# Recurrence: four small LoRA products side by side in the array, and two scalings made by ScalarE

## The chip, the cores and the metric
One core of a Trainium2 chip. The metric is the device time of one execution in microseconds (us), the median of several executions.

## The reference, cut to what matters
Two feed-forward blocks stand around a recurrence ("attn") with 8 batches of 512 tokens and 128 channels, `LORA = 32`. What the change touches, from the recurrence:

```
xm = x + dxa * miu_x
lora_h = tanh(xm @ A_lora).reshape(b, t, 5, -1)
miu = lambda_ + einsum('btfi,fic->fbtc', lora_h, B_lora)
w_in, k_in, v_in, r_in, g_in = x[None] + dxa[None] * miu
y_t = r_t @ (S + u * k_t^T v_t);  S = diag(decay_t) S + k_t^T v_t
yn = groupnorm(y) * gn_gamma + gn_beta
return yn * g @ Wo.T
```

The second LoRA factor is a product with 32 rows of contraction for each of five inputs f (w, k, v, r, g). r times u is an operand of the recurrence's diagonal; the scale and the bias of the group norm are applied to its turned output.

## The kernel before
The program runs in phases, each ended by a barrier of all engines. The recurrence is one phase. It works batch by batch on 128 channels by 512 tokens, in fp32. Each engine has its own instruction stream, and semaphores of the class `Signal` (`wait` for a value made, `free` for a buffer given back) join them.

The parts of the work are named by kind. "mix" makes batch b+1's projections, "scan" does batch b's recurrence in levels of doubling length, "tail" normalises, turns and projects batch b-1, and "next" prepares batch b+2. All engines go through one written order, each taking the parts that it has. There is no planner.

```
ORDER = (("scan", "start"), ("mix", "lora"), ("tail", "norm"), ("scan", "level1"), ("mix", "shift0"),
         ("mix", "mixed0"), ("scan", "level2"), ("mix", "shift1"), ("tail", "turn"), ("mix", "mixed1"),
         ("scan", "level3"), ("mix", "shift2"), ("tail", "out"), ("mix", "td"), ("mix", "mixed2"), ("scan", "level4"),
         ("mix", "shift3"), ("mix", "rate"), ("scan", "level5"), ("mix", "shift4"), ("next", "xm"), ("scan", "far"),
         ("mix", "mixed3"), ("mix", "k"), ("scan", "keys"), ("mix", "mixed4"), ("mix", "v"), ("scan", "state"),
         ("mix", "r"), ("mix", "g"), ("mix", "chain"), ("mix", "first_k"), ("scan", "y"))
```

`batches` (L1476) runs this order once with mix alone, once without tail, then a hardware loop of two turns with two runs each, and four runs more. So there are eight runs with a mix part, eight with a scan part and eight with a tail part.

The lines that matter, by engine:
- TensorE: `mix_lora` (L1791, L1793) makes the first factor, whose tanh ScalarE writes to `lora` (L1705) and `lora4` (L1706). `mix_shift(f)` (L1810) makes the second factor of input f. For f below 4 it multiplies all 128 rows of `lora` by `B_lora[:, f, :]`, which is zero outside the 32 rows of f; for f = 4 it takes 32 rows. The results go to the PSUM banks 2, 3, 0, 1 and again 2. The scan levels are L1859 (64 rows by 32 columns), the far products L1880, `tail_turn` L1918, `tail_out` L1924, the projections td, k, r, g L1785, and rate L1820.
- VectorE: `mix_shift(f)` (L1538) adds lambda and multiplies by dxa. `keep_level` (L1642) copies a level's result under a mask, `next_q` (L1589) scales the queries. `mix_r` (L1546) makes `ru` = q0 times u, once ScalarE has copied r to q0. `mix_g` (L1552) makes the gate from ScalarE's tanh. `mix_chain` (L1566) makes the products of the decay. `tail_turn` makes `yg` = scale times the turned output plus bias (L1627), and then `ygT` = yg times gate (L1631), which `tail_out` on TensorE needs.
- GpSimd: `mixed` (L1662, five in a run), `next_k` (L1681, seven in a run), the group norm's power (L159) and scaling (L165).
- ScalarE: the PSUM copies k (L1730), the turned keys (L1761), seven copies into aT (L1767, L1771), v (L1734), r (L1738), the gate's tanh (L1743), and 14 copies of decay factors (L1755, L1756).

Of the kernel before, what the change touches and what calls it, by code (L numbers as in the profile page):

```python
# [8 lines left out]
ALU = mybir.AluOpType  # L9
ACT = mybir.ActivationFunctionType  # L10
# [1329 lines left out]
LORA = 32  # L1340
# [75 lines left out]
def recurrence_phase(nc, ps, s, x_all, zT):  # L1416
# [8 lines left out]
    with Phase(nc) as ctx:  # L1425
# [14 lines left out]
        dxa, xm, lora, lora4 = sb("dxa", [P, T]), sb("xm", [P, T]), sb("lora", [P, T]), sb("lora4", [LORA, T])  # L1440
# [76 lines left out]
        with nc.Block() as block:  # L1517
            @block.vector
            def _(vec):
                v = nc.vector  # L1520
# [10 lines left out]
                def mix_shift(f):  # L1531
                    def part(b, i):
                        miu_made.wait(vec, b, f + 1)
                        if f >= 2:
                            mixed_ready.wait(vec, b, f - 1)
                        else:
                            mixed_ready.free(vec, b)
                        v.scalar_tensor_tensor(shift[f % 2][:], ps[:, MIU_BANK[f], :], s["lambda"][:, f:f + 1], dxa[:],  # L1538
                                               ALU.add, ALU.mult).then_inc(shift_ready.sem, 1)
                    return part  # L1540

                def mix_r(b, i):
                    r_kept.wait(vec, b)
                    if not isinstance(b, int) or b >= 2:
                        level_made.free(vec, b - 1)
                    v.tensor_scalar(ru[i][:], q0[i][:], s["u"][:, 0:1], None, ALU.mult).then_inc(ru_kept.sem, 1)  # L1546

                def mix_g(b, i):
                    gt_kept.wait(vec, b)
                    if not isinstance(b, int) or b >= 2:  # L1550
# [71 lines left out]
                    gn.variance(vec, b)  # L1622

                def tail_turn(b, i):
                    yn_turned.wait(vec, b)
                    ygT_ready.free(vec, b)
                    v.tensor_scalar(yg[:], ps[:, YT_BANK, :], s["gn_w_half"][:, 0:1], s["gn_b_half"][:, 0:1], ALU.mult,  # L1627
                                    ALU.add).then_inc(yg_ready.sem, 1)
                    yg_ready.wait(vec, b)
                    out_made.free(vec, b)  # L1630
                    v.tensor_tensor(ygT[:], yg[:], gate[i][:], ALU.mult).then_inc(ygT_ready.sem, 1)  # L1631
# [7 lines left out]
                def keep_level(b, l):  # L1639
# [3 lines left out]
                                      ps[:, LEVEL_BANK:LEVEL_BANK + NH, 0:TPB * BLOCK].rearrange("p h (c w) -> p h c w", c=TPB)  # L1643
                                      ).then_inc(level_kept.sem, 1)

                batches(vec, next_xm=next_xm, **{f"mix_shift{f}": mix_shift(f) for f in range(5)}, mix_r=mix_r,
                        mix_g=mix_g, mix_chain=mix_chain, scan_start=scan_start, **{f"scan_level{l}": scan_level(l) for l in range(1, DIAG_LEVELS + 1)},
                        scan_far=scan_far, scan_state=scan_state, scan_y=scan_y,
                        tail_norm=tail_norm, tail_turn=tail_turn, tail_out=tail_out)
# [48 lines left out]
            @block.scalar  # L1698
            def _(act):
                a = nc.scalar  # L1700

                def mix_lora(b, i):
                    lora_made.wait(act, b)
                    miu_made.free(act, b)
                    a.activation(lora[:], ps[:, 0, :], ACT.Tanh).then_inc(lora_kept.sem, 1)  # L1705
                    a.activation(lora4[:], ps[0:LORA, 1, :], ACT.Tanh).then_inc(lora_kept.sem, 1)  # L1706

                def mix_td(b, i):
                    td_made.wait(act, b)
                    w_made.free(act, b)  # L1710
                    a.activation(td_hidden[:], ps[0:HS, TD_BANK, :], ACT.Tanh).then_inc(td_kept.sem, 1)

                def mix_rate(b, i):
                    w_made.wait(act, b)
                    decay_ready.free(act, b)
                    a.activation(rate[:], ps[:, W_BANK, :], ACT.Exp, bias=s["td_miu"][:, 0:1]).then_inc(rate_ready.sem, 1)
                    rate_ready.wait(act, b)
                    if not isinstance(b, int) or b >= 2:
                        factors.free(act, b - 1)
                        chain.free(act, b - 1)  # L1720
                    a.activation(decay[i][:], rate[:], ACT.Exp, scale=-1.0).then_inc(decay_ready.sem, 1)

                def mix_k(b, i):
                    k_made.wait(act, b)
                    if not isinstance(b, int) or b >= 2:
                        level_made.free(act, b - 1)
                        k_next.free(act, b - 1)
                        q_next.free(act, b - 1)
                        y_made.free(act, b - 1)
                    a.activation(k0[i][:], ps[:, K_BANK, :], ACT.Copy).then_inc(k_kept.sem, 1)  # L1730

                def mix_v(b, i):
                    v_made.wait(act, b)
                    a.activation(v_rows[i][:].rearrange("p c w -> p (c w)"), ps[:, V_BANK, :], ACT.Copy).then_inc(v_kept.sem, 1)  # L1734

                def mix_r(b, i):
                    r_made.wait(act, b)
                    a.activation(q0[i][:], ps[:, R_BANK, :], ACT.Copy).then_inc(r_kept.sem, 1)  # L1738

                def mix_g(b, i):  # L1740
                    g_made.wait(act, b)
                    g_kept.free(act, b)
                    a.activation(gate_tanh[:], ps[:, G_BANK, :], ACT.Tanh, scale=0.5).then_inc(gt_kept.sem, 1)  # L1743

                def mix_chain(b, i):
                    for l in range(LEVELS):
                        src = decay[i] if l == 0 else block_decay[l - 1]
                        pairs = src[:].rearrange("p (n two) -> p n two", two=2)
                        if l:
                            chain.wait(act, b, l)  # L1750
                        else:
                            decay_ready.wait(act, b)
                            q_next.free(act, b)
                            k_next.free(act, b)
                        a.activation(q_factor[l][:, :, 1], pairs[:, :, 0], ACT.Copy)  # L1755
                        a.activation(k_factor[l][:, :, 0], pairs[:, :, 1], ACT.Copy).then_inc(factors.sem, 1)  # L1756

                def scan_keys(b, i):
                    kT_made.wait(act, b)
                    kv_made.free(act, b)  # L1760
                    a.activation(kT[:].rearrange("p c w -> p (c w)"), ps[:, KT_BANK, :], ACT.Copy).then_inc(kT_kept.sem, 1)  # L1761
                    far_made.wait(act, b)
                    y_made.free(act, b)
                    bank = LEVEL_BANK
                    far = ps[:, bank:bank + NH, :].rearrange("p h (c t) -> p h c t", c=TPB)
                    for at, to in ((slice(0, 32), slice(32, 64)), (slice(64, 96), slice(96, 128)), (slice(0, 64), slice(64, 128))):
                        a.activation(aT[at, :, :, to], far[at, :, :, to], ACT.Copy).then_inc(far_kept.sem, 1)  # L1767
                    level_kept.wait(act, b)
                    for q in range(P // BLOCK):
                        at = slice(q * BLOCK, (q + 1) * BLOCK)  # L1770
                        a.activation(aT[at, :, :, at], diag[at, :, :, :], ACT.Copy).then_inc(near_kept.sem, 1)  # L1771

                def scan_y(b, i):
                    gn.squares(act, b)

                batches(act, mix_lora=mix_lora, mix_td=mix_td, mix_rate=mix_rate, mix_k=mix_k, mix_v=mix_v, mix_r=mix_r,
                        mix_g=mix_g, mix_chain=mix_chain, scan_keys=scan_keys, scan_y=scan_y)

            @block.tensor
            def _(pe):  # L1780
                t = nc.tensor
# [10 lines left out]
                    k_kept.free(pe, b)  # L1792
                    t.matmul(ps[0:LORA, 1, :], s["A_lora"][:, P:], xm[:], start=True, stop=True).then_inc(lora_made.sem, 1)  # L1793

                def mix_shift(f):
                    def part(b, i):
                        if f == 0:
                            lora_kept.wait(pe, b)

                            r_kept.free(pe, b)  # L1800
                            ru_kept.free(pe, b)
                        elif f == 1:
                            v_kept.free(pe, b)
                        elif f == 4:
                            shift_ready.wait(pe, b, 1)
                        if f == 4:
                            lhsT, rhs = s["B_lora4"][:], lora4[:]
                        else:
                            lhsT, rhs = s["B_lora"][:, f, :], lora[:]
                        t.matmul(ps[:, MIU_BANK[f], :], lhsT, rhs, start=True, stop=True).then_inc(miu_made.sem, 1)  # L1810
                    return part

                def mix_td(b, i):
                    shift_ready.wait(pe, b, F_K + 1)
# [106 lines left out]
                def tail_out(b, i):  # L1921
                    ygT_ready.wait(pe, b)
                    for c in range(TPB):
# [1 line left out]
                                        start=True, stop=True)  # L1925
                    last.then_inc(out_made.sem, 1)

                batches(pe, mix_lora=mix_lora, **{f"mix_shift{f}": mix_shift(f) for f in range(5)}, mix_td=mix_td,
                        mix_rate=mix_rate, mix_k=mix_k, mix_v=mix_v, mix_r=mix_r, mix_g=mix_g,
                        scan_start=scan_start, **{f"scan_level{l}": scan_level(l) for l in range(1, DIAG_LEVELS + 1)},  # L1930
                        scan_far=scan_far, scan_keys=scan_keys, scan_state=scan_state, scan_y=scan_y,
# [96 lines left out]
```

## Time and profile before
| | us |
|---|---|
| median of 3 runs | 1597.56 |
| lowest and highest of them | 1591.68, 1601.63 |
| the profiled execution, its own time | 1610.69 |
| its span, first to last instruction | 1608.9 |
| PE, DVE, ACT, POOL busy over the span | 1292.8, 1121.5, 877.7, 698.0 |
| TensorE's mean granted clock | 0.867 |

PE is TensorE's matmuls, PEld its weight loads, DVE VectorE, ACT ScalarE, POOL GpSimd. A busy time is a union of intervals. The granted clock is a share of full speed: 1.00 is 2.4 GHz, 0.50 is 1.2 GHz. The profile's own page cuts the span into 40 equal slices of 40 us, too coarse for the recurrence, which lies between about 685 and 955 us. The sections below therefore use its windows, its groups by line and its timeline.

### The profile page before, as it was taken

To read this page: it belongs to the slowest core of one execution; us is meant where nothing else is said; L and a number is where in the kernel's file an instruction comes from. 1 tells how busy PE (TensorE), PEld (TensorE's weight loads), DVE (VectorE), ACT (ScalarE), POOL (GpSimd) and SP (SyncE) were. 2 spreads that over 40 slices of the span, in tenths; PEclk is the share of its full clock that TensorE was granted. 3 is DMA by queue.
4 is the path that set the end of the run, shared out by engine and by line. 5 is a ranking of instruction groups with operands and counts; after the bars stand their busy time and mean duration, and the time that the engine had idled before them with its cause. 6 is when DMAs were issued, how large, how long until landed. Compare 5 with 4: busy or idle time off the path is not lost. (4 is left out here: it accounts for less than half of the span.)

```text
span 1608.9 us, 39937 instructions
## 1 busy us (share of the span) xinstructions
PE 1292.8 (80%) x12720; PEld 732.9 (46%) x12721; DVE 1121.5 (70%) x1736; ACT 877.7 (55%) x1782; POOL 698.0 (43%) x817
## 2 busy tenths in 40 slices
PE   3579999999978397278788745489999999976693
PEld 2324444434458397125445433234444444476593
DVE  7678888888736232758788759588889888463232
ACT  3438888888841153224334314168888888820351
POOL 5433333333336365246566625513333333336462
PEclk9769999999975599589899858689999999965797
DMA  3421433211100121100000002512111111001224
GB/s 111 167 57 43 112 91 78 62 49 48 29 1 30 48 68 51 41 2 2 3 2 2 3 1 105 150 36 51 45 54 46 48 53 45 12 1 43 62 68 117
DMA packets 81641, 81.93 MB, mean 51 GB/s; under 512 B 16265, under 2 KB 53868, under 8 KB 81536
## 3 DMA queue, kind: packets, MB, share of 16 engines
q1 hardware_dynamic: 72704, 70.01, 15.6%
q0 software_dynamic: 4608, 8.44, 1.6%
q10 hardware_dynamic: 4224, 2.10, 0.4%
q8 instruction: 64, 1.05, 0.3%
q14 instruction: 41, 0.34, 0.1%
HBM read 50.56 MB, written 29.93 MB: 50 GB/s over the span
## 5 line engine op out<-in xcount | busy, mean ns | idle before, releaser
L795 DVE TENSOR_REDUCE maxima<-ps 128x2 f32<-128x1024 f32 x512 | 624.1, 1226 | 88.1 <-PE ps L624 83.1
L777 ACT ACTIVATE probs<-ps 128x512 f32<-128x512 f32 x1024 | 553.1, 593 | 87.0 <-PE ps L651 69.7
L624 PE MATMUL ps<-k_stack,q_stack 62*128 62x512 f32 x1024 | 385.8, 476 | 36.6 <-DMA k_stack<-k_split 25.5
L651 PE MATMUL ps<-q_stack,k_stack 64*128 64x512 f32 x1024 | 390.0, 459 | 0.3
L661 PE MATMUL ps<-probs,v_stack 128*32 128x256 f32 x4096 | 327.5, 392 | 1.1 <-ACT probs L777 1.0
L590 POOL TENSOR_TENSOR inv<-o_rows,minus_one 128x16 f32<-128x16 f32 x64 | 186.3, 2911 | 237.4 <-ACT o_rows L758 237.4
L624 PEld LDWEIGHTS ps<-k_stack,q_stack 62*128 62x128 f32 x1024 | 157.7, 193 | 229.7 <-issue 115.9
L651 PEld LDWEIGHTS ps<-q_stack,k_stack 64*128 64x128 f32 x1024 | 159.3, 186 | 17.0 <-issue 7.3
L661 PEld LDWEIGHTS ps<-probs,v_stack 128*32 128x32 f32 x4096 | 80.9, 108 | 171.7 <-issue 112.2
L1275 POOL DMA_INDIRECT expert_out<-yt,number x80 | 78.7, 984 | 69.0 <-issue 44.4
L1233 ACT ACTIVATE xT<-ps,ln_b,ln_w 128x128 f32<-128x128 f32 x80 | 36.6, 458 | 107.2 <-PE ps L1204 105.1
L1252 DVE COPY w_now<-w 128x512 f32 x80 | 34.4, 430 | 77.8 <-issue 41.6
L1210 PE MATMUL ps<-xT,w_now 128*128 128x128 f32 x640 | 88.4, 283 | 0.1
L1217 PE MATMUL ps<-w,hidT 128*128 x640 | 84.9, 276 | 0.0
L1210 PEld LDWEIGHTS ps<-xT,w_now 128*128 128x128 f32 x640 | 80.6, 198 | 0.4 <-issue 0.3
L583 POOL CAST neg_wide<-maxima 128x16 fp32r<-128x16 f32 x64 | 12.7, 198 | 155.1 <-DVE maxima L795 155.1
L1217 PEld LDWEIGHTS ps<-w,hidT 128*128 128x128 f32 x640 | 78.4, 193 | 0.1
L1133 POOL DMA_INDIRECT sorted<-rows,slot x64 | 62.2, 972 | 26.5 <-issue 16.4
L1238 ACT ACTIVATE hidT<-ps 128x512 f32<-128x512 f32 x80 | 47.8, 598 | 36.4 <-PE ps L1210 35.8
L1681 POOL TENSOR_TENSOR r_kx<-r_kx,r_k_factor 128x512 f32<-128x512 f32 x48 | 60.6, 1263 | 13.0 <-PE ps L1859 9.6
L1662 POOL TENSOR_TENSOR r_mixed<-r_shift,zT 128x512 f32<-128x512 f32 x40 | 57.1, 1436 | 19.0 <-DVE r_shift L1538 19.0
L420 PE MATMUL ps<-hT,w_qkv 128*128 128x512 f32 x64 | 44.7, 837 | 17.4 <-ACT hT L384 17.4
(215 smaller groups left out, 1843.8 us busy)
## 6 DMA issues: line engine op xcount, KB each, us to landing
q_stack<-q_split SPq DMA_DIRECT2D x256, 64.0 KB
k_stack<-k_split SPq DMA_DIRECT2D x512, 32.0 KB
q_split<-q_parts SPq DMA_DIRECT2D x16, 512.0 KB, 2.8
k_split<-k_parts SPq DMA_DIRECT2D x16, 512.0 KB, 3.6
xt<-sorted SPq DMA_DIRECT2D x80, 64.5 KB
w<-in_L_ffn_w SPq DMA_DIRECT2D x16, 256.0 KB, 3.0
rows<-expert_out SPq DMA_DIRECT2D x16, 256.0 KB, 3.2
x_all<-in_L_attn_x SPq DMA_DIRECT2D x8, 256.0 KB, 3.0
```

The lines of the kernel that those rows point to most:

```text
L590: g_.tensor_tensor(inv[:], o_rows[:, :, :, DK], minus_one[:], ALU.pow).then_inc(inv_ready, 1)
L624: mm = t.matmul(psS[:, h, :], qs[g][score_rows(h), h // 2, u * P:(u + 1) * P], ks[g][score_rows(h), h // 2, :], start=True, stop=True)
L651: t.matmul(ring("e", u, n), ks[g][half(h), h // 2, u * P:(u + 1) * P], qs[g][half(h), h // 2, :], start=True, stop=True).then_inc(e_ready, 1)
L661: last = t.matmul(psO[VW * h:VW * (h + 1), here], vs[g][:, u, h, :], probs[u % 2][:, h, here], start=(u == 0 and part == 0), stop=(u == TP ...
L777: a.activation(probs[u % 2][:, h, :], ring("e", u, n), ACT.Exp, scale=float(DK) ** -0.5).then_inc(e_read, 1)
L795: v.tensor_reduce(maxima[i][:, :, pair, u:u + 1], psS[:, 2 * pair:2 * pair + 2, :], AX_X, ALU.max, negate=True).then_inc(s_read, 1)
L1133: pool.indirect_dma_start(xs, bass.IndirectOffsetOnAxis(ap=slot[:, i:i + 1], axis=0), rows[:, i, :], None).then_inc(scattered, 16)
L1210: last = t.matmul(psH[o][:, c * P:(c + 1) * P], w1_now[o][:, c * P:(c + 1) * P], xT[o][:], start=True, stop=True)
L1217: last = t.matmul(psY[i][:, 0:P], hidT[i][:, c, :], s["w2"][:, ds(second_expert, 1), c, :], start=(c == 0), stop=(c == HC - 1))
L1275: pool.indirect_dma_start(ys, bass.IndirectOffsetOnAxis(ap=number[out_slot][:], axis=0), yt[out_slot][:], None, bounds_check=TOK - 1, oob_ ...
L1662: g.tensor_tensor(mixed[f][:], shift[f % 2][:], x, ALU.add).then_inc(mixed_ready.sem, 1)
L1681: g.tensor_tensor(dst[:].rearrange("p (k m) -> p k m", m=m), src[:].rearrange("p (k m) -> p k m", m=m), k_factor[l][:].rearrange("p n two ...
```

## The change
TensorE's parts shift0 to shift3 become one part at shift0: four matmuls, each with the 32 rows of its own f of weights and of `lora`, one behind the other in the queue, to four different banks. They wait at the top for all that the four waited for. VectorE still takes shift0 to shift3 in their old places. VectorE's `ru` goes to ScalarE, from PSUM, behind the copy of r; VectorE's `yg` goes to ScalarE, from PSUM. The number of matmuls stays the same.

```diff
@@ VectorE
-                def mix_r(b, i):
-                    r_kept.wait(vec, b)
-                    if not isinstance(b, int) or b >= 2:
-                        level_made.free(vec, b - 1)
-                    v.tensor_scalar(ru[i][:], q0[i][:], s["u"][:, 0:1], None, ALU.mult).then_inc(ru_kept.sem, 1)
...
                 def tail_turn(b, i):
-                    yn_turned.wait(vec, b)
-                    ygT_ready.free(vec, b)
-                    v.tensor_scalar(yg[:], ps[:, YT_BANK, :], s["gn_w_half"][:, 0:1], s["gn_b_half"][:, 0:1], ALU.mult,
-                                    ALU.add).then_inc(yg_ready.sem, 1)
                     yg_ready.wait(vec, b)
                     out_made.free(vec, b)
                     v.tensor_tensor(ygT[:], yg[:], gate[i][:], ALU.mult).then_inc(ygT_ready.sem, 1)
@@ ScalarE
                 def mix_r(b, i):
                     r_made.wait(act, b)
                     a.activation(q0[i][:], ps[:, R_BANK, :], ACT.Copy).then_inc(r_kept.sem, 1)
+                    if not isinstance(b, int) or b >= 2:
+                        level_made.free(act, b - 1)
+                    a.activation(ru[i][:], ps[:, R_BANK, :], ACT.Copy, scale=s["u"][:, 0:1]).then_inc(ru_kept.sem, 1)
...
+                def tail_turn(b, i):
+                    yn_turned.wait(act, b)
+                    ygT_ready.free(act, b)
+                    a.activation(yg[:], ps[:, YT_BANK, :], ACT.Identity, bias=s["gn_b_half"][:, 0:1],
+                                 scale=s["gn_w_half"][:, 0:1]).then_inc(yg_ready.sem, 1)
@@ TensorE
+                def mix_shift0(b, i):
+
+                    lora_kept.wait(pe, b)
+                    r_kept.free(pe, b)
+                    ru_kept.free(pe, b)
+                    v_kept.free(pe, b)
+                    for f in range(4):
+                        at = slice(f * LORA, (f + 1) * LORA)
+                        t.matmul(ps[:, MIU_BANK[f], :], s["B_lora"][at, f, :], lora[at, :],
+                                 start=True, stop=True).then_inc(miu_made.sem, 1)
+
+                def mix_shift4(b, i):
+                    shift_ready.wait(pe, b, 1)
+                    t.matmul(ps[:, MIU_BANK[4], :], s["B_lora4"][:], lora4[:], start=True, stop=True).then_inc(miu_made.sem, 1)
```

## Rows read from the trace of the kernel before
**Rows 1.** Window: busy us (instructions) of PE, PEld, DVE, ACT, POOL; granted clock, DMA share, GB/s.
```profile
685.00:955.00 270.00, 210.28 (x4064) 123.65 (x4064) 202.50 (x344) 93.51 (x257) 150.86 (x130) 0.87 0.01 2
```

**Rows 2.** Groups by line, 685 to 960 us: count | busy, mean ns | idle before.
```profile
L1810 PE MATMUL ps<-r_lora,B_lora 128*128 128x512 f32 x64 | 40.8, 728 | 3.8 <-ACT r_lora L1706 3.8
...
L1627 DVE TENSOR_SCALAR r_yg<-ps,gn_w_half,gn_b_half 128x512 f32<-128x512 f32 x8 | 6.4, 801 | 4.8 <-PE ps L1918 4.8
...
L1716 ACT ACTIVATE r_rate<-ps,td_miu 128x512 f32<-128x512 f32 x8 | 5.5, 688 | 15.8 <-PE ps L1820 15.8
...
L1546 DVE TENSOR_SCALAR r_ru<-r_q,u 128x512 f32<-128x512 f32 x8 | 3.9, 487 | 7.1 <-ACT r_q L1738 7.1
```

**Rows 3.** Timeline of POOL, one ordinary run: start, us, what, count [idle before].
```profile
743.29 1.16 POOL L1681 TENSOR_TENSOR r_kx<-r_kx,r_k_factor 128x512 f32<-128x512 f32 x1
744.40 1.73 POOL L1662 TENSOR_TENSOR r_mixed<-r_shift,zT 128x512 f32<-128x512 f32 x1
746.10 1.09 POOL L1681 TENSOR_TENSOR r_kx<-r_kx,r_k_factor 128x512 f32<-128x512 f32 x1
...
753.51 1.05 POOL L1681 TENSOR_TENSOR r_kx<-r_kx,r_k_factor 128x512 f32<-128x512 f32 x1 [0.47 <-PE ps L1859]
```

**Rows 4.** Timeline of DVE, the same run.
```profile
740.87 0.68 DVE L1589 TENSOR_TENSOR r_qx<-r_qx,r_q_factor 128x512 f32<-128x512 f32 x1
...
743.67 1.33 DVE L1589 TENSOR_TENSOR r_qx<-r_qx,r_q_factor 128x512 f32<-128x512 f32 x1
...
753.62 0.44 DVE L1642 COPY_PREDICATED r_diag<-level_masks,ps 128x256 f32<-128x256 int32 x1 [0.83 <-PE ps L1859]
...
762.36 0.48 DVE L1546 TENSOR_SCALAR r_ru<-r_q,u 128x512 f32<-128x512 f32 x1 [0.70 <-ACT r_q L1738]
762.87 0.69 DVE L1552 SCALAR_TENSOR_TENSOR r_gate<-r_gate_tanh,ps 128x512 f32<-128x512 f32 x1
```

**Rows 5.** Timeline of PE, the same run.
```profile
742.83 0.28 PE L1859 MATMUL ps<-r_qx,r_kx 64*32 64x32 f32 x12 [0.79 <-issue]
...
755.26 0.68 PE L1880 MATMUL ps<-r_qx,r_kx 64*64 64x64 f32 x16 [0.40 <-DVE r_qx L1589]
755.87 1.13 PE L1785 MATMUL ps<-r_mixed,WkT 128*128 128x512 f32 x2
```

**Rows 6.** Timeline of ACT, the same run.
```profile
757.25 0.60 ACT L1730 ACTIVATE r_k<-ps 128x512 f32<-128x512 f32 x1 [2.97 <-PE ps L1785]
...
761.73 0.59 ACT L1738 ACTIVATE r_q<-ps 128x512 f32<-128x512 f32 x1
762.21 0.60 ACT L1743 ACTIVATE r_gate_tanh<-ps 128x512 f32<-128x512 f32 x1
```

**Rows 7.** Timeline, a later ordinary run: POOL's first key product and PE's second far product.
```profile
835.81 1.60 POOL L1681 TENSOR_TENSOR r_kx<-r_kx,r_k_factor 128x512 f32<-128x512 f32 x1
...
846.99 0.68 PE L1880 MATMUL ps<-r_qx,r_kx 64*64 64x64 f32 x16 [0.62 <-DVE r_qx L1589]
```

**Rows 8.** Timeline of POOL, the run at the loop's turn.
```profile
813.39 1.09 POOL L1662 TENSOR_TENSOR r_mixed<-r_shift,zT 128x512 f32<-128x512 f32 x1 [1.42 <-DVE r_shift L1538]
...
816.82 1.05 POOL L1681 TENSOR_TENSOR r_kx<-r_kx,r_k_factor 128x512 f32<-128x512 f32 x1 [1.33 <-PE ps L1859]
```

**Rows 9.** Timeline of PE in the attention phase: two row halves at work.
```profile
1101.27 0.50 PE L624 MATMUL ps<-k_stack,q_stack 62*128 62x512 f32 x1
1101.28 0.73 PE L651 MATMUL ps<-q_stack,k_stack 64*128 64x512 f32 x2
1101.62 0.40 PE L624 MATMUL ps<-k_stack,q_stack 62*128 62x512 f32 x1
```

**Rows 10.** Windows around one fall of the clock, the columns as in rows 1.
```profile
766.30:769.70 3.40, 1.41 (x67) 0.81 (x66) 3.21 (x8) 1.82 (x6) 0.00 (x1) 1.00 0.00 0
769.50:773.50 4.00, 3.94 (x68) 1.77 (x69) 2.88 (x6) 0.00 (x1) 3.62 (x3) 0.57 0.02 4
```

**Rows 11.** Timeline of PE, last scan: tail_out at the lower clock.
```profile
924.99 2.08 PE L1924 MATMUL ps<-WoT,r_ygT 128*128 128x128 f32 x8 [0.85 <-DVE r_ygT L1631]
```

More of the change, by code:

```diff
@@ L1644, in keep_level @@
                                       ).then_inc(level_kept.sem, 1)
-                batches(vec, next_xm=next_xm, **{f"mix_shift{f}": mix_shift(f) for f in range(5)}, mix_r=mix_r,
+                batches(vec, next_xm=next_xm, **{f"mix_shift{f}": mix_shift(f) for f in range(5)},
                         mix_g=mix_g, mix_chain=mix_chain, scan_start=scan_start, **{f"scan_level{l}": scan_level(l) for l in range(1, DIAG_LEVELS + 1)},
@@ L1774, in scan_y @@
                     gn.squares(act, b)
+                def tail_turn(b, i):
[3 more added lines that the diff above has]
+                                 scale=s["gn_w_half"][:, 0:1]).then_inc(yg_ready.sem, 1)
                 batches(act, mix_lora=mix_lora, mix_td=mix_td, mix_rate=mix_rate, mix_k=mix_k, mix_v=mix_v, mix_r=mix_r,
-                        mix_g=mix_g, mix_chain=mix_chain, scan_keys=scan_keys, scan_y=scan_y)
+                        mix_g=mix_g, mix_chain=mix_chain, scan_keys=scan_keys, scan_y=scan_y,
+                        tail_turn=tail_turn)
             @block.tensor
@@ L1793, in mix_lora @@
                     t.matmul(ps[0:LORA, 1, :], s["A_lora"][:, P:], xm[:], start=True, stop=True).then_inc(lora_made.sem, 1)
[L1795 to L1811, printed above, removed]
+                def mix_shift0(b, i):
[10 more added lines that the diff above has]
+                    t.matmul(ps[:, MIU_BANK[4], :], s["B_lora4"][:], lora4[:], start=True, stop=True).then_inc(miu_made.sem, 1)
                 def mix_td(b, i):
@@ L1926, in tail_out @@
                     last.then_inc(out_made.sem, 1)
-                batches(pe, mix_lora=mix_lora, **{f"mix_shift{f}": mix_shift(f) for f in range(5)}, mix_td=mix_td,
+                batches(pe, mix_lora=mix_lora, mix_shift0=mix_shift0, mix_shift4=mix_shift4, mix_td=mix_td,
                         mix_rate=mix_rate, mix_k=mix_k, mix_v=mix_v, mix_r=mix_r, mix_g=mix_g,
```

## The prediction
> **What bounds the kernel now.** I read the window over the recurrence first, then its groups by line, then the timeline of one ordinary run, engine by engine, and last the windows for the clock. The recurrence is 270 us of 1608.9, 17% of the span, and in it PE is busy 210.28 us and DVE 202.50 us [rows 1]. Eight full runs, a start and an end fill it, so a run takes about 29 us. Neither engine is full, so the bound must be looked for as a chain that closes from run to run. I follow it from gate to gate.
>
> In the ordinary run of rows 3 to 6 the chain goes like this. The gate starts at 762.87 [rows 4]. Behind the gate before it DVE works without a gap, up to the group norm's variance. POOL then makes the power and the scaled tile. After that comes the stage that matters: POOL's first key product starts at 743.29 [rows 3], and PE's second far product starts at 755.26 [rows 5]. This stage lasts 11.97 us. Then PE makes k at 755.87 [rows 5], and ACT works from 757.25 to the end of the gate's tanh, 762.21 + 0.60 = 762.81 [rows 6], in one unbroken row of copies. DVE's gate at 762.87 needs that tanh.
>
> What fills the stage of 11.97 us? Look at DVE's query product (L1589): it takes 0.68 us at 740.87, with POOL in its small power operation, and 1.33 us at 743.67, behind a POOL product that ends at 744.45 [rows 3, 4]. 743.67 + 1.33 = 745.00 is 0.55 after that end. And POOL's mixed at 744.40 takes 1.73 us, ending 1.13 after 745.00, which is what such an operation takes alone (1.09) [rows 3, 8]. So products of two SBUF tensors on DVE and POOL's products take turns, each waiting for the other to end. In the stage there are five key products at 1.05, three mixed at 1.08 and five DVE products (four queries and ygT), each adding about 0.55: 5.25 + 3.24 + 2.75 = 11.24 us. A later run needed only 846.99 - 835.81 = 11.18 us [rows 7]. The stage is thus full except for short gaps, and its floor is about 11.2 us. PE's work and DVE's reads of PSUM run under it.
>
> **The change part by part.**
>
> *The four shifts.* They remove from PE three slots, at shift1 to shift3. The weight of one: 64 records of 128 rows, two per matmul, are busy 40.8 us, so 1.27 us per matmul over both clocks [rows 2]. That is 3 x 1.27 = 3.8 us of PE per run, 30 us in all, if the four run at once in the time of one. That two row groups run at once is seen in the attention phase: L624 and L651 start 0.01 us apart, in halves of 62 and 64 rows, and all four passes are over at 1102.02, after 0.75 us [rows 9]. Four quarters are not in the trace. Bounds for the four: 1.27 us (all at once) and 5.1 us (one after another). I take 1.27, by rows 9. The same rows weigh on the order in the queue. The second passes start together at 1101.62, behind both first passes, although each matmul's two passes are neighbours in the program. A pass of the second matmul did not wait for the first's second pass. The Trainium skill ("TensorE: Matmul & The Clock Gate", Part 2: What happens when you issue a matmul) says that the matmuls themselves stay in program order and only weight loads are pulled ahead; by that rule first and second passes of four row groups would overlap only pairwise, five slots for eight passes. It is a rival below.
>
> What PE's relief is worth is read from the stage. Where it waits for PE it shortens: POOL waited 0.47 for level 5, DVE 0.83 for the same level, and PE's rate and level 5 sit behind shift3 [rows 3, 4]. But the stage cannot fall under 11.2. So: the ordinary run shown gains 11.97 - 11.2 = 0.77, the one of rows 7 nothing, and of the five ordinary runs the other three lie at or between these (0.75, 0.85, 0.1 by the same subtraction): 2.5 us together. In the run at the loop's turn PE was slow and POOL stood 1.42 us for shift2 and 1.33 for level 5 [rows 8]; together 2.75, of which I count 1.5, since level 5 still needs td and rate. The two first runs stand on waits of DVE and PE which the move touches little: 0.35 each, 0.7. There the fetch-like stall of 0.79 in level 2 [rows 5] stays where it is. Sum 4.7 us. Bounds: nothing and 8 us (each of seven runs saving the 0.83 at level 5, and 2.75 at the turn).
>
> *yg on ACT.* DVE loses 8 x 0.801 = 6.4 us [rows 2]. ACT has nothing between the two tanhs of lora and that of td, so its copy hides; it lasts about 0.69, as an activation from PSUM with a column as bias does [rows 2], and two crossings between engines come in. DVE can reach ygT earlier by up to 0.8, but ygT is one of the five that take turns with POOL. It changes places, not the sum. yg reads PSUM and took 0.80 each time. Worth 0 inside the stage; in the last two tails, where no mix runs, 0.15 together. Bounds: -0.3 and 6.4.
>
> *ru on ACT.* DVE loses 8 x 0.487 and a wait of 7.1 us for q0 [rows 2]. Neither was on the chain: ru ended at 762.84 and the tanh at 762.81 [rows 4, 6]. On ACT ru stands between q and the tanh, inside the unbroken row. Activations of this size follow one another there at 762.21 - 761.73 = 0.48 us [rows 6]; I take 0.50 for the one with a column as scale, and 0.69 as the upper end [rows 2]. The tanh is later by that, and with it the gate, the chain of decays, the group norm and level 0. Eight runs: +4.0 us, bounds 0 and 5.5. DVE now idles in front of the gate. Behind the tanh are queued the 14 decay copies, and POOL's first key product waits for the second of them; its result is first needed at level 2 of the next run. TensorE's level 0 waits for ru, ready before its y products end.
>
> *Waits gathered at shift0.* r_kept, ru_kept and v_kept belong to the run before, whose copies end before its y products: nothing.
>
> **Sum.** -4.7 - 0.15 + 4.0 = -0.85, say -0.9 us. The profiled execution would go from 1610.69 to 1609.8. It is 13.1 us above the median of 1597.56, so I carry the difference over: 1596.7. The runs before spread over 10 us; about 1% (16 us) is what a measurement of this kernel tells from no change.
>
> **The rivals.**
>
> *DVE bounds the recurrence.* Then all that it loses counts: 6.4 + 3.9 + 7.1 = 17.4 us, and the time is 1580.2. For it: DVE at 75% and busiest in most windows after PE. Against it: the taking of turns, which is left with as many members, and DVE's wait for ACT before each ru, in eight of eight runs. Chance 0.08.
>
> *The four don't run at once.* Level 2 comes 3.8 us later. The first key product and the first mixed run meanwhile, until 746.10 [rows 3], so about 1 us per run is left, +8: 1604.7. For it: no trace of four. Against it: rows 9. Chance 0.07.
>
> *They overlap pairwise only.* Five slots of 0.64 are 3.2 us instead of 1.27, so level 2 is 1.9 later; at half a us per run that makes +4, 1600.7. This is what the Trainium skill's rule on program order, cited above, would give. Chance 0.05, since rows 9 show the other order.
>
> *The clock falls (slower).* PE was busy 1.41 us of 3.4 from 766.30, and from 769.50 the granted clock was 0.57, with the first shift at 1.94 us [rows 10]: the level of 1.2 GHz after little work. With shift1 and shift2 gone PE does little between level 2 and tail_out, turn and level 3, by my estimate 1.4 us in 4.5 (four transposes and one level as now). If the clock falls there in each run, tail_out takes 2.08 us [rows 11] instead of 1.04, td and rate 1 us more each, so 3 us by level 5, against 1.4 us of room: +1.6 in six or seven runs, +10 us, 1607. If it stayed low, the work of PE, 210 - 25 = 185 us at a mean of 0.87, would be 322 us at 0.50 and outlast the 270: +52, 1649. It decides from where PE's work between two gates, at the clock it gets, exceeds the run's 29 us. Against it: DVE and POOL drive PE every 2 us. Chance 0.13, of which 0.05 for more than 1% slower.
>
> **How the numbers follow.** The forecast has 0.67. Range 1586 to 1607: the unknown costs make -8.15 (1589.4) to 0.3 + 5.5 = +5.8 (1603.4), to which I add 3 us at both ends for the spread of a median; the clock's first price lies at the upper end, 1607, and the first rival's time and the clock's second lie outside. Faster by over 1%: 0.08 (the first rival); slower by over 1%: 0.05; within: 0.87.
>
> **What would show it.** Right: the three later shifts gone from PE's timeline, the four records of shift0 starting within a few hundredths; the stage at 11.0 to 11.4 us in every ordinary run; DVE's wait before the gate at 1.0 us or more, ended by ACT; gate to gate still 28.5 to 29.3; DVE's busy time in the recurrence about 10 us lower for nothing. Wrong: a stage well under 11 us (the turns are not the bound), a gate no later behind q than now, shift0's records spread over 3 us, or granted clocks of 0.5 to 0.7 between level 2 and td in most runs.

## The result and the profile after

| | before | changed |
|---|---|---|
| median of 6 runs, us | 1597.24 | 1608.49 |
| lowest and highest, us | 1591.43, 1601.63 | 1606.07, 1612.87 |
| the profiled execution's own time, span, us | 1610.69, 1608.9 | 1612.87, 1611.1 |
| mean granted clock over the span | 0.867 | 0.845 |

The ratio is 1.0078 with an interval of 1.0051 to 1.0106: slower by 11 to 12 us, 1.5 us beyond the upper end of the range.

The profiled executions differ by only 2.2 us, because the phases ahead of the recurrence happened to be 6.1 us shorter in the changed kernel's profile (the first xm starts at 683.20 instead of 689.30) and the phases behind it another 6.1. Those phases are the same code in both, so I compare the recurrence itself, cut at the same two points. It was 273.1 us (681.0 to 954.1) and is 287.5 us. Windows of the changed kernel (columns as in rows 1): the whole recurrence, its first run, and two neighbouring stretches in one ordinary run:

```profile
674.90:962.40 287.50, 213.55 (x4064) 128.94 (x4064) 192.73 (x330) 104.39 (x273) 150.93 (x132) 0.74 0.01 2
684.00:708.50 24.50, 19.74 (x97) 7.00 (x98) 6.99 (x10) 7.98 (x14) 6.26 (x6) 0.55 0.00 1
741.20:745.20 4.00, 1.54 (x68) 1.19 (x68) 3.57 (x4) 0.78 (x1) 4.00 (x4) 0.78 0.01 4
745.40:749.60 4.20, 4.17 (x42) 2.34 (x43) 2.83 (x4) 0.09 (x1) 4.20 (x4) 0.50 0.01 2
```

The same stretches of the kernel before (the whole phase, its first run, and the stretches around the same level and tail_out):

```profile
681.00:954.10 273.10, 210.28 (x4064) 123.65 (x4064) 202.80 (x346) 93.51 (x257) 151.72 (x132) 0.87 0.01 2
690.00:708.80 18.80, 16.82 (x96) 5.92 (x96) 7.19 (x11) 7.30 (x12) 5.83 (x6) 0.79 0.00 1
742.50:746.50 4.00, 3.48 (x84) 1.93 (x83) 3.14 (x5) 0.00 (x0) 4.00 (x4) 1.00 0.01 4
746.50:750.90 4.40, 3.21 (x76) 2.10 (x76) 4.25 (x6) 0.59 (x1) 4.40 (x4) 1.00 0.01 2
```

The column of the granted clock, the last but two, tells the story. As many matmuls run, DVE has 10 us less to do, and the granted clock is 0.74 instead of 0.87. Ahead of tail_out PE is busy 1.54 of 4.00 us where it was busy 3.48, and the next stretch is granted 0.50, which is 1.2 GHz, where it was 1.00, 2.4 GHz. The timeline of PE in that ordinary run of the changed kernel:

```profile
739.02 1.14 PE L1803 MATMUL ps<-r_lora,B_lora 32*128 32x512 f32 x8 [0.43 <-ACT r_lora L1696]
740.10 0.76 PE L1856 MATMUL ps<-r_qx,r_kx 64*32 64x32 f32 x64
742.09 0.66 PE L1915 MATMUL ps<-ident,r_yn 128*128 128x128 f32 x4 [1.23 <-POOL r_yn L165]
743.93 0.88 PE L1856 MATMUL ps<-r_qx,r_kx 64*32 64x32 f32 x64 [1.19 <-POOL r_kx L1671]
745.42 2.07 PE L1921 MATMUL ps<-WoT,r_ygT 128*128 128x128 f32 x8 [0.61 <-DVE r_ygT L1621]
747.43 1.97 PE L1785 MATMUL ps<-r_mixed,td_A 128*64 128x512 f32 x2
749.33 0.89 PE L1856 MATMUL ps<-r_qx,r_kx 64*32 64x32 f32 x64
750.23 1.13 PE L1817 MATMUL ps<-r_td_hidden,td_B 64*128 64x512 f32 x2
...
753.88 0.68 PE L1877 MATMUL ps<-r_qx,r_kx 64*64 64x64 f32 x16 [0.17 <-DVE r_qx L1583]
```

The four matmuls of shift0 are the first line: eight records in 1.14 us. PE then waits 1.23, 1.19 and 0.61 us for others, where shift1 and shift2 stood, and tail_out and td take 2.07 and 1.97 us. Groups by line of the changed kernel (columns as in rows 2), 674 to 964 us:

```profile
L1921 PE MATMUL ps<-WoT,r_ygT 128*128 128x128 f32 x64 | 15.7, 422 | 8.6 <-DVE r_ygT L1621 8.6
L1785 PE MATMUL ps<-r_mixed,td_A 128*64 128x512 f32 x16 | 14.8, 1028 | 2.5 <-POOL r_mixed L1652 2.2 <-DVE r_shift L1538 0.3
L1785 PE MATMUL ps<-r_mixed,WkT 128*128 128x512 f32 x16 | 13.2, 921 | 0.0
...
L1803 PE MATMUL ps<-r_lora,B_lora 32*128 32x512 f32 x64 | 12.5, 863 | 3.6 <-ACT r_lora L1696 3.6
```

The kernel before had for the first three:

```profile
L1924 PE MATMUL ps<-WoT,r_ygT 128*128 128x128 f32 x64 | 11.0, 324 | 6.7 <-DVE r_ygT L1631 6.7
L1785 PE MATMUL ps<-r_mixed,td_A 128*64 128x512 f32 x16 | 8.5, 616 | 0.1
L1785 PE MATMUL ps<-r_mixed,WkT 128*128 128x512 f32 x16 | 9.0, 645 | 0.0
```

The same products, tail_out, td and k, cost 4.7, 6.3 and 4.2 us more. The four shifts went from 40.8 [rows 2] to 12.5 us, and still PE's busy time rose.

ACT and DVE at the end of that run:

```profile
760.35 0.59 ACT L1728 ACTIVATE r_q<-ps 128x512 f32<-128x512 f32 x1
760.96 0.69 ACT L1731 ACTIVATE r_ru<-ps,u 128x512 f32<-128x512 f32 x1
761.55 0.59 ACT L1736 ACTIVATE r_gate_tanh<-ps 128x512 f32<-128x512 f32 x1
```
```profile
762.17 0.69 DVE L1546 SCALAR_TENSOR_TENSOR r_gate<-r_gate_tanh,ps 128x512 f32<-128x512 f32 x1 [1.78 <-ACT r_gate_tanh L1736]
```

From q to the tanh it is 1.20 us, before it was 0.48 [rows 6]; DVE stands 1.78 us in front of the gate.

**Where the 14.4 us of the two profiles lie**, cut at the gates. From the first xm to the first gate 24.09 us instead of 18.76: +5.3, of which ru is about 0.2 (from q to the tanh it is 1.13 us there instead of 0.90). From the first to the eighth gate 212.96 instead of 203.93: +9.0. Ahead and behind: nothing. Each of the seven intervals between these gates has three pieces. From the gate to the first key product they sum to 63.1 us instead of 64.1: -1.0. The stages (first key product to second far product) sum to 87.25 us instead of 86.86, so they give +0.4 where -4.7 was forecast. Behind the second far product it is 62.6 instead of 53.0: +9.6, of which ru is 7 x 0.72 = 5.0. The other 4.5 or so lie where the k product stands: it takes 1.77 to 2.07 us in four of the seven intervals of the changed kernel, and 1.13 in all seven of the kernel before.

### The profile page after: what moved, and what is told of

It reads as the page before. It is cut to its first block and busy times, and to the rows that moved or that the text cites. A ratio compares the mean times of both kernels' runs of the same rounds, so it can differ in the third digit from the quotient of the medians.

```text
span 1611.1 us, 39938 instructions
## 1 busy us (share of the span) xinstructions
PE 1297.1 (81%) x12720; PEld 739.9 (46%) x12721; DVE 1111.5 (69%) x1720; ACT 888.4 (55%) x1798; POOL 696.4 (43%) x817
## 5 line engine op out<-in xcount | busy, mean ns | idle before, releaser
L583 POOL CAST neg_wide<-maxima 128x16 fp32r<-128x16 f32 x64 | 12.5, 196 | 153.7 <-DVE maxima L795 153.7
```

## The experiments

All kernels ran beside the kernel before on their own chip, whose median was 1597, 1611 or 1612 us by chip; the ratios are to that. "Recurrence" is cut as above. "Slow k" says in how many of the seven intervals between the gates the k product took 1.6 us or more; elsewhere it takes 1.1. Clock, recurrence, slow k and the last column are of one profile each. "Fillers" are matmuls that write to a PSUM bank whose content nobody reads before it is written anew; nothing of the computation is left out by them.

| kernel | ratio [95%] | recurrence, us | clock | slow k | first xm to first gate |
|---|---|---|---|---|---|
| before | | 273.1 | 0.87 | 0 | 18.76 |
| changed | 1.0078 [1.0051, 1.0106] | 287.5 | 0.74 | 4 | 24.09 |
| pe_only | 1.0105 [1.0071, 1.0139] | 286.5 | 0.77 | 6 | 21.77 |
| act_only | 1.0025 [1.0004, 1.0047] | 275.8 | 0.83 | 2 | 19.31 |
| fill | 1.0039 [1.0016, 1.0061] | 280.6 | 0.82 | 5 | 22.0 |
| serial4 | 1.0092 [1.0058, 1.0126] | 287.1 | 0.83 | 2 | 17.98 |
| pe_fill3 | 0.9990 [0.9966, 1.0013] | 272.1 | 0.86 | 2 | 17.54 |
| fill3 | 1.0021 [0.9997, 1.0046] | 278.4 | 0.83 | 4 | 19.8 |
| fill3_ru_dve | 0.9984 [0.9957, 1.0010] | 271.0 | 0.88 | 3 | 17.46 |
| yg_only | 1.0007 [0.9988, 1.0026] | 272.6 | 0.86 | 3 | 18.79 |
| fill4_ru_dve | 0.9975 [0.9950, 1.0000] | 269.5 | 0.89 | 0 | 17.89 |
| before_fill | 1.0000 [0.9978, 1.0021] | 273.2 | 0.87 | 2 | 17.83 |
| ru_dve | 1.0023 [0.9994, 1.0053] | 281.0 | 0.78 | 3 | 23.12 |
| after_again | 1.0087 [1.0063, 1.0111] | 281.7 | 0.77 | 1 | 22.85 |

**pe_only: TensorE's part alone.** VectorE's `mix_r` and `tail_turn` are as before. Against the kernel before, the body of `mix_shift0` is that of the change, and:

```diff
-                batches(pe, mix_lora=mix_lora, **{f"mix_shift{f}": mix_shift(f) for f in range(5)}, mix_td=mix_td,
+                batches(pe, mix_lora=mix_lora, mix_shift0=mix_shift0, mix_shift4=mix_shift4, mix_td=mix_td,
```

> Only TensorE's part of the change: the four shifts side by side at shift0; ru and yg stay on VectorE. Clock theory (TensorE, relieved, is granted 1.2 GHz in more stretches, and its later matmuls then hold up the stage): the first run still takes 24 us from xm to gate instead of 18.8, stages of 11.9 to 13.5 us remain, and the kernel is slower than before by 4 to 10 us. ScalarE theory (the loss is ru and yg on ScalarE): no slower than before, rather 3 to 5 us faster, since the loop's turn gains about 3 us.

1628.21 against 1611.88 us. Windows of pe_only, the recurrence and the two stretches around tail_out, and PE's timeline there:

```profile
684.80:971.30 286.50, 209.30 (x4064) 129.46 (x4064) 202.36 (x346) 93.92 (x257) 149.46 (x132) 0.77 0.01 2
750.10:754.10 4.00, 1.54 (x68) 1.19 (x68) 3.96 (x5) 0.00 (x0) 4.00 (x4) 0.86 0.02 6
754.30:758.50 4.20, 4.19 (x42) 2.35 (x43) 2.81 (x4) 0.10 (x1) 4.20 (x4) 0.50 0.00 0
```
```profile
754.31 2.08 PE L1921 MATMUL ps<-WoT,r_ygT 128*128 128x128 f32 x8 [0.45 <-DVE r_ygT L1631]
756.32 1.97 PE L1785 MATMUL ps<-r_mixed,td_A 128*64 128x512 f32 x2
```

The part that only takes work from PE costs 16 us (13.4 in the profile) by itself, as much as the whole change within the two intervals. The direction is that of the clock theory; the size is not, for 4 to 10 us were expected. Again 1.54 of 4.00 us busy, then 0.50. In six of the seven intervals the k product is slow too:

```profile
764.04 2.07 PE L1785 MATMUL ps<-r_mixed,WkT 128*128 128x512 f32 x2
```

**act_only: ru and yg on ScalarE, TensorE as before.** Against the changed kernel:

```diff
-                batches(pe, mix_lora=mix_lora, mix_shift0=mix_shift0, mix_shift4=mix_shift4, mix_td=mix_td,
+                batches(pe, mix_lora=mix_lora, **{f"mix_shift{f}": mix_shift(f) for f in range(5)}, mix_td=mix_td,
```

> Only the two moves to ScalarE; TensorE's shifts stay in their four places over 128 rows. Clock theory: TensorE's work and clock are as before, so only the tanh behind ru counts: 8 x 0.64 us from the changed kernel's rows (ru from 706.02, tanh from 706.66), +3 to +5 us. ScalarE theory: the whole loss of the change, +11 us.

1617.90 against 1611.88, which is 6.0 us by the medians; the ratio makes it +4.0. The latter lies within the forecast. TensorE's clock did not stay as it was, though: 0.83, with the k product slow in two intervals, although TensorE has the same work as before.

**fill: the changed kernel with unread matmuls in the places of shift1 and shift2.** Against the changed kernel:

```diff
+                def mix_filler(b, i):
+                    for _ in range(1):
+                        t.matmul(ps[:, OUT_BANK, :], s["B_lora"][:, 0, :], lora[:], start=True, stop=True)
...
-                batches(pe, mix_lora=mix_lora, mix_shift0=mix_shift0, mix_shift4=mix_shift4, mix_td=mix_td,
+                batches(pe, mix_lora=mix_lora, mix_shift0=mix_shift0, mix_shift4=mix_shift4, mix_shift1=mix_filler, mix_shift2=mix_filler, mix_td=mix_td,
```

> The changed kernel plus one matmul of 128 rows by 512 columns, whose result nobody reads, at each of the old places shift1 and shift2 (into the bank of the output product, free there). No dependence is touched, TensorE only gets work back. Clock theory: the granted clock of the recurrence returns to 0.87 or more, tail_out and td take 1.1 us each instead of 2, the first run takes 19 us from xm to gate, and the kernel gains 6 to 12 us over the changed one: 1597 to 1602. Any theory without the clock: the fillers can only cost, 0 to +4 us over the changed kernel.

1618.81 against 1611.88, about 6 us less than the changed kernel by the ratios, with more work on PE. Tail_out is back at full clock, the later k product is not:

```profile
757.74 1.16 PE L1926 MATMUL ps<-WoT,r_ygT 128*128 128x128 f32 x8
758.83 1.07 PE L1785 MATMUL ps<-r_mixed,td_A 128*64 128x512 f32 x2
766.23 1.71 PE L1785 MATMUL ps<-r_mixed,WkT 128*128 128x512 f32 x2
```

The first run stays slow too, 22.0 us where 19 was expected. A filler in the third place, shift3, was tried next, in pe_fill3, fill3, fill3_ru_dve and fill4_ru_dve.

**serial4: the four at shift0, each over all 128 zero-padded rows.** Against the changed kernel:

```diff
-                        t.matmul(ps[:, MIU_BANK[f], :], s["B_lora"][at, f, :], lora[at, :],
+                        t.matmul(ps[:, MIU_BANK[f], :], s["B_lora"][:, f, :], lora[:],
```

> The changed kernel, but the four matmuls at shift0 take all 128 rows of zero-padded weights, so that they run one behind the other in the same early place. If the early place alone helped, with the clock kept up by work: clock as before (0.87), level 2 some 3.2 us later in every run, which costs 0.5 to 1 us per run, +4 to +8 us over before by the placing and +4 for ru: 1603 to 1609. If low clock is the greater cost, it lies at or below the changed kernel's 1608 although it does 3.2 us more TensorE work per run. If side by side is what matters, it lies above 1612.

1627.63 against 1611.88. The windows of serial4 over the recurrence and its first run, and PE there:

```profile
676.50:963.60 287.10, 217.64 (x4064) 130.71 (x4064) 187.84 (x330) 104.31 (x273) 149.42 (x132) 0.83 0.01 2
686.00:704.00 18.00, 15.29 (x97) 5.36 (x97) 7.08 (x10) 7.91 (x14) 6.26 (x6) 0.90 0.00 1
```
```profile
690.70 3.70 PE L1803 MATMUL ps<-r_lora,B_lora 128*128 128x512 f32 x8 [1.15 <-ACT r_lora L1696]
694.33 1.07 PE L1785 MATMUL ps<-r_mixed,td_A 128*64 128x512 f32 x2
```

The whole time does not tell the theories apart, as two effects meet. In the first run the longer block keeps the full clock: 0.90 instead of 0.55, and 17.98 us to the first gate instead of 24.09, although the shifts take 3.70 us there and not 2.09. It does not bring it. The clock was already at 1.00 when the block began, where the changed kernel's was at 0.50. The fair comparison is after_again, the changed kernel's second profile, whose short block also ran at 1.00. Windows of the short block and of the stretch behind it:

```profile
688.40:689.70 1.30, 1.14 (x8) 0.31 (x8) 0.09 (x1) 0.00 (x0) 0.00 (x0) 1.00 0.01 6
690.50:703.90 13.40, 11.42 (x19) 4.69 (x20) 4.92 (x6) 4.38 (x6) 5.75 (x5) 0.50 0.00 1
```

Behind the short block the clock fell; behind the long one it did not, and td took 1.07 us. In the ordinary runs of serial4 the block delays level 2 and the stages are 12.2 to 14.1 us. The four 32-row matmuls take 2.09 us in the first run and 1.14 in an ordinary one; the four of 128 rows take 3.70 in the first run, at clock 1.00, and 4.74 in an ordinary one (at 738.77), at 0.77. At full clock that is 1.14 against 3.70 us: the packing is real.

**pe_fill3: pe_only with three fillers.** This is the experiment that settles the cause: TensorE's part as changed, with its holes filled. Against pe_only:

```diff
+                def mix_filler(bank):
+                    return lambda b, i: t.matmul(ps[:, bank, :], s["B_lora"][:, 0, :], lora[:], start=True, stop=True)
...
+                ... mix_shift1=mix_filler(OUT_BANK), mix_shift2=mix_filler(OUT_BANK), mix_shift3=mix_filler(KV_BANK), ...
```

> TensorE's part of the change alone (as in pe_only: 286.5 us of recurrence against 273.1 before), plus three matmuls of 128 by 512 whose results nobody reads, at the old places shift1, shift2 and shift3, so that TensorE has about as much work as before, and the four shifts are early. Clock theory: all of the 13.4 us is clock, so the recurrence returns to 270 to 275 us and the whole to within 4 us of before. If something else in side-by-side matmuls costs (a drain between tilings, the queue), it stays at 280 or more.

1608.72 against 1610.82. The same three windows:

```profile
682.50:954.60 272.10, 211.28 (x4112) 124.88 (x4112) 200.27 (x346) 93.73 (x257) 152.86 (x132) 0.86 0.01 2
742.70:746.70 4.00, 2.63 (x72) 1.38 (x70) 3.97 (x5) 0.00 (x0) 4.00 (x4) 1.00 0.02 6
746.90:751.10 4.20, 4.20 (x78) 2.44 (x78) 3.83 (x7) 0.59 (x1) 4.20 (x4) 1.00 0.02 4
```

48 more matmul records, and the recurrence is 14.4 us shorter than pe_only's; the clock stays at 1.00 through both stretches. Nothing else differs, so the fall of the clock is what pe_only pays. Of the 14.4 us, 4.2 lie in the first run, 4.7 in the stages and 6.1 behind them, where the k product is slow in two intervals instead of six; the rest, -0.5, is ahead of the stages. What PE's saved time would be worth at a held clock this does not show, since the fillers take that time back (PE is busy 211.28 us, before 210.28).

**fill3: the changed kernel with the same three fillers**, and **fill3_ru_dve: that with ru back on VectorE.**

```diff
@@ VectorE, fill3_ru_dve only
+                def mix_r(b, i):
+                    ...
+                    v.tensor_scalar(ru[i][:], q0[i][:], s["u"][:, 0:1], None, ALU.mult).then_inc(ru_kept.sem, 1)
@@ ScalarE, fill3_ru_dve only
-                    a.activation(ru[i][:], ps[:, R_BANK, :], ACT.Copy, scale=s["u"][:, 0:1]).then_inc(ru_kept.sem, 1)
```

> The changed kernel plus the same three matmuls (fill had two: 280.6 us of recurrence, K and V still at half speed behind shift4). Clock theory: the third removes most of what was left, recurrence 275 to 278, of which 4 to 5 us are ru on ScalarE; the whole +2 to +5 us over before. If two were enough, no gain over fill: 280 to 282.

> As fill3, but ru goes back to VectorE, yg stays on ScalarE. Theory (ru on ScalarE stands in the chain to the gate, 0.6 us per run; yg costs nothing there): 4 to 5 us under fill3, recurrence 269 to 273, the whole 0 to 5 us under before. Rival (yg's crossings cost as much as ru): within 2 us of fill3.

1615.57 and 1607.75 against 1610.82. Windows of fill3, then of fill3_ru_dve:

```profile
686.80:965.20 278.40, 218.60 (x4112) 128.65 (x4112) 183.35 (x330) 104.60 (x273) 155.06 (x132) 0.83 0.01 2
```
```profile
681.90:952.90 271.00, 208.74 (x4112) 124.16 (x4112) 194.69 (x338) 100.06 (x265) 153.66 (x132) 0.88 0.01 2
```

Ru's place is worth 7.4 us of recurrence here, 7.8 in the medians and 6.0 by the ratios. Of the 7.4, 5.1 lie in the seven intervals, about 7 x 0.72. The other 2.3 lie in the first run and go with the clock, which stays at 0.50 until 705.4 in fill3 (10.4 us behind the first xm) and until 694.1 in fill3_ru_dve (3.9 us behind it).

**yg_only: yg on ScalarE, all else as before.**

```diff
@@ VectorE
-                    v.tensor_scalar(yg[:], ps[:, YT_BANK, :], s["gn_w_half"][:, 0:1], s["gn_b_half"][:, 0:1], ALU.mult,
-                                    ALU.add).then_inc(yg_ready.sem, 1)
@@ ScalarE
+                    a.activation(yg[:], ps[:, YT_BANK, :], ACT.Identity, bias=s["gn_b_half"][:, 0:1],
+                                 scale=s["gn_w_half"][:, 0:1]).then_inc(yg_ready.sem, 1)
```

> The kernel before with only yg moved to ScalarE. Theory: worth nothing or a little, since ygT changes places in the taking of turns and TensorE's clock is untouched: recurrence 271 to 274, the whole -2 to +1 us. act_only (yg and ru) had 275.8, so ru's share is the difference, 2 to 5 us. Rival (VectorE bounds): 6 us faster.

1611.72 against 1610.82, recurrence 272.6: no difference. The working is subtler than the forecast had it. Its stages sum to 83.05 us, 3.8 less than before, with TensorE's program untouched, yet its seven intervals sum to 203.39, only 0.5 less. From the second far product to the gate it is 8.52 us in one ordinary run instead of 755.26 to 762.87 = 7.61 [rows 4, 5]: what the stage gives, the part behind it takes back. That is the clock again. The expectation had TensorE's clock untouched, but the k product, 1.13 us before [rows 5], is slow in three of the seven intervals, and these three hold the 3.4 us that the part behind the stages lost. In that ordinary run:

```profile
761.15 1.87 PE L1788 MATMUL ps<-r_mixed,WkT 128*128 128x512 f32 x2
```

**fill4_ru_dve: the best version found**, with a fourth filler behind the first LoRA factor, and **before_fill: that filler in the kernel before.**

```diff
                     t.matmul(ps[0:LORA, 1, :], s["A_lora"][:, P:], xm[:], start=True, stop=True).then_inc(lora_made.sem, 1)
+                    t.matmul(ps[:, YT_BANK, :], s["ident"][:], xm[:], start=True, stop=True)
```

> fill3_ru_dve (recurrence 271.0 us, clock 0.88) plus one more matmul of 128 by 512 behind lora, where TensorE waits 1.5 us for level 0's copy, into the bank that is free there. Its result is read by nobody. Clock theory: the falls that follow that wait go, clock 0.92 or more, K and V take 1.1 us each in every run: recurrence 266 to 270, the whole 3 to 8 us under before. Rival (what is left in K and V comes from the gap in front of far, or costs nothing): recurrence 271 to 273.

> The kernel before plus that one matmul behind lora and nothing of the change. Clock theory: it removes the fall at 769 us and the one at 861 us and shortens the one at the loop's turn; since the stage hides most of it, recurrence 270 to 273 against 273.1, the whole -3 to 0 us. If matmuls cost what they take when nothing waits: +0 to +2.

1607.98 and 1613.15 against 1612.23. The recurrence window of fill4_ru_dve and three of its products, the last of which was 1.71 us in fill:

```profile
680.50:950.00 269.50, 214.09 (x4128) 123.71 (x4128) 193.59 (x338) 99.70 (x265) 153.68 (x132) 0.89 0.01 2
```
```profile
744.85 1.05 PE L1928 MATMUL ps<-WoT,r_ygT 128*128 128x128 f32 x8
745.84 1.07 PE L1788 MATMUL ps<-r_mixed,td_A 128*64 128x512 f32 x2
...
753.22 1.12 PE L1788 MATMUL ps<-r_mixed,WkT 128*128 128x512 f32 x2
```

Four us better than before, with an interval that touches 1. The clock is 0.89 where 0.92 was expected, but of the changed variants this is the only one whose k product is at 1.1 us in all seven intervals, and in it the shorter stages (82.6 us) stay a gain: the recurrence is 3.6 us under before. In the kernel before, the filler does nothing for the time. Yet its stages shorten as well, to 84.0 us, with more work on PE, and the k product is then slow twice.

**ru_dve: the changed kernel with ru on VectorE, no filler.** The edit is that of fill3_ru_dve without the fillers.

```diff
-                batches(vec, next_xm=next_xm, **{f"mix_shift{f}": mix_shift(f) for f in range(5)},
+                batches(vec, next_xm=next_xm, **{f"mix_shift{f}": mix_shift(f) for f in range(5)}, mix_r=mix_r,
```

> The changed kernel with ru back on VectorE and no filler: side by side and yg on ScalarE. Clock theory: the clock's price stays (pe_only 286.5 us of recurrence), yg is worth nothing: 283 to 287, the whole 10 to 17 us over before. If ru on ScalarE were the change's loss: 274 or less.

1616.37 (1599.85 to 1624.76) against 1612.23, recurrence 281.0 at clock 0.78. A miss: it should have been 10 to 17 us over before, as pe_only is, and is +3.7 us by the ratio. It differs from pe_only in yg alone, which did nothing in yg_only. In this profile the k product is slow in three intervals where pe_only has six.

**after_again: the changed kernel once more**, on a chip where before is 1596.76.

> The changed kernel itself once more, as a measure of how far a recurrence's length depends on the execution: its falls of the clock are set off by gaps of a few us. Theory: they recur in most runs, recurrence 283 to 289 us with a granted clock of 0.74 to 0.78, the whole 8 to 16 us over before. If the first profile was a chance draw: recurrence under 280 and a ratio under 1.004.

1609.82, +13 us. The recurrence in this profile is 281.7 us at 0.77, not 287.5 at 0.74:

```profile
674.50:956.20 281.70, 207.57 (x4064) 126.19 (x4064) 191.48 (x330) 104.04 (x273) 150.21 (x132) 0.77 0.01 2
```

So one profile of a kernel whose clock falls can be some 6 us off another in this phase, though the result repeats. Tail_out is about as slow in both; the k product is slow in one interval here and in four there, and behind the stages that makes 3.6 us of the 5.8. The gap between ru_dve and pe_only (5.5 us) is of that size.

## Why the prediction was wrong

**The step that failed** is the choice among the cases. "The clock falls" was a rival with 0.13; it is what happened. Its working named one place and the sign: little PE work between level 2 and tail_out, then tail_out at 2.08 and td 1 us longer; measured 2.07 and 1.97, and tail_out is that slow in five of the six runs that have a mix part beside it. Its first price, 1607, is near the 1608.49, but that is luck. It put +10 us into the stages, at 1.6 each, where the changed kernel shows +0.4 and pe_only +2.1. The rest was paid in places that it did not name, the first run and the k product behind the stage. What argued it down, "DVE and POOL drive PE every 2 us", was no row of the trace. Rows 10 were: 1.41 of 3.4 us busy, and 0.57 behind it. My own estimate of the new stretch, 1.4 us in 4.5, was a smaller share than that, and the measured one is 1.54 in 4.00. The row that should have weighed most was the one I cited for the size. pe_only and pe_fill3 show the cause: 14.4 us of recurrence for 24 unread matmuls. The range could not have caught it either: its upper end stood on this rival's first price, and its lower end left out the bound of 6.4 that the text gives for yg.

**Its point of decision was wrong as well.** It said that the clock matters from where PE's work exceeds the run's 29 us. PE was busy 213.55 of 287.50 us, never full; at half clock its links in the chain just take longer.

**The four shifts, -4.7 us.** That four run at once in the time of one is right: 1.14 us for eight records, against 1.12 for one matmul of 128 rows. In the trace the first passes of all four start at 739.02 to 739.04 and the second passes at 739.56 to 739.58. The Trainium skill ("TensorE: Matmul & The Clock Gate", Part 2) says that matmuls stay in program order. Read as a rule for the single passes of an fp32 matmul, as the prediction read it, it would give five slots, and this row contradicts that reading. The floor is right too: most ordinary stages of fill3, fill3_ru_dve and yg_only are 11.12 to 11.36 us, and a floor of 11.2 was worked out from turns of DVE and POOL. But as a gain the term is not there in the changed kernel: its stages came to +0.4. Nor does a shorter stage show a relief of PE. Yg_only and before_fill have stages 3.8 and 2.9 us shorter with as much work on PE or more, and the slow k products behind the stages took 3.4 and 2.1 us of it back. The sum counted a stage's shortening one for one; that was the second error. What the relief alone is worth at a held clock no run shows.

**The first run** was priced at a gain of 0.35. It lost 5.3 us, 0.2 of it by ru, at clock 0.55 instead of 0.79. PE in the first run of the kernel before:

```profile
695.17 4.25 PE L1810 MATMUL ps<-r_lora,B_lora 128*128 128x512 f32 x6 [1.15 <-ACT r_lora L1706]
699.48 1.04 PE L1785 MATMUL ps<-r_mixed,td_A 128*64 128x512 f32 x2
```

Three 128-row shifts in a row, 4.25 us, stood there, and td behind them ran at 1.04 us. In serial4 and pe_fill3, where a block or fillers stand, the run is 17.98 and 17.54 us. That these are below 18.76 says little: in both the clock was at 1.00 before the shifts began, and in the kernel before it rose only within them. No case named this place.

**ru, +4.0 us.** The mechanism was right, the size was off: 0.72 per run and not 0.50, but only 0.2 in the first run, where ACT's row has gaps; so 5.3 us, just within its upper bound of 5.5. The 0.72 come about since ru starts 0.61 us behind q and the tanh 0.59 behind ru, where the tanh followed q after 0.48. Three measures by difference give 3.2 (act_only less yg_only), 7.4 (fill3 less fill3_ru_dve) and 0.7 to 6.5 us (the changed kernel's two profiles less ru_dve).

**yg, -0.15 us,** and **the waits gathered at shift0, 0:** nothing in the runs speaks against either (yg_only 1.0007).

**DVE bounds the recurrence:** refuted. DVE lost 10 us of work and stood in front of the gate instead, 1.78 us in the run shown, as forecast.

**What stays open.** The parts don't add up: in the profiles TensorE's part alone is +13.4, with yg +7.9, with ru as well +8.6 and +14.4. Single profiles scatter by about as much here. Part of the scatter goes with the count of slow k products, six, three, one and four in these profiles; why the clock falls ahead of one k product and not of the next was not tested, nor whether yg on ScalarE helps there. Why the phases ahead of the recurrence differ between executions wasn't looked into.

## What to carry to other kernels
Before taking matmuls from an engine that is not full, look at the windows around the place: which granted clock follows a stretch of that little work, and which products of the chain would then run at 1.2 GHz. Where a change of TensorE's order slows a kernel, put unread matmuls into the holes; read with the granted clock, that is a quick test of whether the clock is the cause, and sometimes the repair. And a copy moved to another engine is free only where that engine's row has a gap: between back-to-back activations it cost 0.72 us, its whole length of 0.69 and a bit more.

## What the hardware showed that I had not expected
Less work on PE made others' waits for it longer: in pe_only four matmuls run in the time of one, and tail_out and td took nearly twice as long. Adding 24 matmuls per execution of the phase made it 14.4 us shorter.

Fp32 matmuls of four different row groups, issued one behind the other, finished in the time of one, both passes of each included: 1.14 us at 2.4 GHz, and in the first run, at 1.2 GHz, the same eight records took

```profile
689.08 2.09 PE L1803 MATMUL ps<-r_lora,B_lora 32*128 32x512 f32 x8 [1.15 <-ACT r_lora L1696]
```

Behind an activation that scales by a column the next one starts 0.59 us later at 128x512, behind a copy 0.48.

A shorter stage can cost what it gives. In yg_only and before_fill three and two k products behind shortened stages ran at the lower clock, where the kernel before had none.
